# Experts of a gated mixture: high weights against high and low rows in one matmul, and a regrouped activation

## The reference

```python
h = jax.nn.silu(jnp.einsum('ech,ehi->eci', inp, wg)) * jnp.einsum('ech,ehi->eci', inp, wu)
out = jnp.einsum('eci,eih->ech', h, wd)
```

## Time and profile before

| | |
|---|---|
| median of three runs | 1830.35 us |
| the profiled execution | 1828.74 us |
| its span, first to last instruction | 1827.0 us |
| TensorE matmuls busy | 1797.5 us, 98% |
| VectorE busy | 1440.9 us, 79% |
| ScalarE busy | 1231.7 us, 67% |
| GpSimd busy | 1064.1 us, 58% |
| mean granted TensorE clock | 0.996 |

### The profile page before, as it was taken

One profiled execution on the slowest core, in us unless ns is written; L12 is line 12 of the kernel. 1 busy time (PEld: TensorE's weight loads), 2 busy tenths in 40 slices (PEclk: granted clock), 3 DMA queues, 4 the chain that ended last, 5 costly groups with the idle time before them and its releaser, 6 DMA issues.

```text
span 1827.0 us, 37430 instructions
## 1 busy us (share of the span) xinstructions
PE 1797.5 (98%) x13271; PEld 1323.8 (72%) x13335; DVE 1440.9 (79%) x2387; ACT 1231.7 (67%) x1799; POOL 1064.1 (58%) x813
## 2 busy tenths in 40 slices
PE   9999998999999999999999999999999999999997
PEld 4666667777777777777777777777777777777775
DVE  5999998787778787777777777777777787777772
ACT  6999997666666666666666666666666666666662
POOL 1101003767677767666666666667667767666651
PEclk9999999999999999999999999999999999999998
DMA  7677764999989999999999999999999999999982
GB/s 247 220 257 248 253 234 171 305 307 306 307 303 309 309 304 299 296 299 297 298 297 298 297 300 299 302 303 308 307 304 308 308 304 297 299 297 297 299 279 46
DMA packets 95817, 516.99 MB, mean 283 GB/s; under 512 B 17696, under 2 KB 22816, under 8 KB 71840
## 3 DMA queue, kind: packets, MB, share of 16 engines
q1 hardware_dynamic: 47968, 357.19, 49.2%
q0 software_dynamic: 42912, 151.04, 35.4%
q10 hardware_dynamic: 4896, 8.26, 1.6%
HBM read 409.21 MB, written 107.22 MB: 283 GB/s over the span
## 4 chain that ended last, share of the span: by engine, by line
PE 81%; DVE 2%; issue 1%; ACT 0%; DMA 0%; POOLq 0%; DVEq 0%; ACTq 0%
PE ps_gu L551 54%; PE ps_d L565 27%; DVE split_g L1161 0%; DVE split_u L1166 0%; DVE split_d L1171 0%; DMA xg<-h_rows,g_idx 0%; DVE xt L1187 0%; DVE xT L1192 0%; ACT ob L837 0%; PE ps_x L533 0%; PE ps_l L447 0%; ACT xT L817 0%; DVE prod L1179 0%; POOLq L106 0%; DVE act L1181 0%
## 5 line engine op out<-in xcount | busy, mean ns | idle before, releaser
L1333 POOL DMA_INDIRECT xg<-h_rows,g_idx x504 | 725.2, 1439 | 188.1 <-issue 134.1
L551 PE MATMUL ps_gu<-xT,split_g 128*128 128x256 bf16 x4608 | 534.1, 273 | 0.8 <-DVE xT L1221 0.8
L551 PE MATMUL ps_gu<-xT,split_u 128*128 128x256 bf16 x4608 | 534.1, 273 | 0.0
L565 PE MATMUL ps_d<-split_d,act 128*128 128x512 bf16 x2240 | 494.3, 379 | 5.4 <-DVE act L1181 1.5
L551 PEld LDWEIGHTS ps_gu<-xT,split_g 128*128 128x128 bf16 x4608 | 450.8, 98 | 66.6 <-issue 1.1
L551 PEld LDWEIGHTS ps_gu<-xT,split_u 128*128 128x128 bf16 x4608 | 450.9, 98 | 52.2
L565 PEld LDWEIGHTS ps_d<-split_d,act 128*128 128x128 bf16 x2304 | 225.1, 98 | 260.9 <-DVE act L1181 2.6
L837 ACT ACTIVATE ob<-ps_d,wcol 128x512 f32<-128x512 f32 x256 | 173.1, 688 | 337.7 <-PE ps_d L565 296.3
L1353 POOL DMA_INDIRECT out<-ob,s_idx x128 | 205.5, 1605 | 291.7 <-ACT ob L837 245.8
L1171 DVE TENSOR_TENSOR split_d<-raw_d,split_d 128x1536 bf16<-128x1536 f32 x128 | 219.2, 1754 | 94.0 <-ACT split_d L809 94.0
L1187 DVE STREAM_TRANSPOSE xt<-xg 128x512 f32<-128x512 f32 x252 | 163.9, 689 | 129.7 <-DMA xg<-h_rows,g_idx 129.7
(11 more groups left out here) (121 smaller groups left out, 1397.4 us busy)
## 6 DMA issues: line engine op xcount, KB each, us to landing
raw_d<-in_wd SPq DMA_DIRECT2D x63, 1536.0 KB
raw_g<-in_wg SPq DMA_DIRECT2D x62, 1536.0 KB
raw_u<-in_wu SPq DMA_DIRECT2D x62, 1536.0 KB
h_rows<-hrow SPq DMA_DIRECT2D x33, 640.0 KB, 3.5
xb<-in_x SPq DMA_DIRECT2D x32, 512.0 KB, 5.3
out<-xb SPq DMA_DIRECT2D x32, 512.0 KB, 3.8
xg<-h_rows,g_idx POOLq DMA_INDIRECT x504
ctx_sb<-in_ctxT SPq DMA_DIRECT2D x8, 512.0 KB, 6.1
```

What stands on the lines that cost most here:

```text
L551: mm = pe.matmul(ps_gu[m][:, t, :], w[:, wi, k, m * P:(m + 1) * P], xT[u][:, k, xi, :], start=(k == 0 and (wi, xi) == (0, 0)), stop=(k == ...
L565: mm = pe.matmul(ps_d[n][:], act[u][:, ai, m, half * P:(half + 1) * P], split_d[:, wi, m, c * NH:(c + 1) * NH], start=(m == 0 and (wi, ai) ...
L1333: p.indirect_dma_start(out=xg[u][:, g, :], out_offset=None, in_=h_rows, in_offset=bass.IndirectOffsetOnAxis(ap=g_idx[u][:, g:g + 1].bitcas ...
```

## The change

- In a gate or up half, the high weights now meet high and low rows in one matmul of 512 columns that fills a whole bank, high x high in its first 256 columns and high x low in the last. The third product, low x high, stays a matmul of 256 columns into the first half. A half is 8 matmuls of 512 and 8 of 256.
- So each half needs a bank: five banks `ps_gu` are used in turn, bank (2m + t) mod 5, and `ps_d` has three, piece 3 using the bank of piece 0. The last up half waits until the first gate is summed; piece 3 waits until piece 0 is read out.
- The two 256-column halves of a bank have to be summed. For the gate, ScalarE copies the second half to `sil` (`gate_part`), VectorE adds the first (`gate_sum`), and ScalarE applies silu to `sil` in place. For the up product, VectorE sums both halves with a `tensor_reduce` into `prod`, and multiplies `prod` by `sil` in place. gate and up halves now signal separately.
- VectorE's low parts of the next expert's gate weights all come after the third activation, ahead of those of the up weights; ScalarE's turned high parts 2 and 3 come after silu 1.
- 20 matmuls in place of 44 run on the identity before the first expert, the first turned rows go to other banks, and near the end of the attention two steps of VectorE for the router's weights go between steps of the routes.

```diff
@@ TensorE
+                if m == MI - 1 and t == 1:
+                    pe.wait_ge(gate_summed, MI * e + 1)
-                    for wi, xi in PAIRS:
-                        mm = pe.matmul(ps_gu[m][:, t, :], w[:, wi, k, m * P:(m + 1) * P], xT[u][:, k, xi, :],
...
+                    pe.matmul(out_ps[:].rearrange("p x c -> p (x c)"), w[:, 0, k, m * P:(m + 1) * P],
+                              xT[u][:, k].rearrange("p x c -> p (x c)"), start=(k == 0), stop=False)
+                    mm = pe.matmul(out_ps[:, 0], w[:, 1, k, m * P:(m + 1) * P], xT[u][:, k, 0], start=False, stop=(k == KH - 1))
+                mm.then_inc((gate_done, up_done)[t], 1)
...
                 for n in range(2, 4):
-                    if not first:
-                        pe.wait_ge(down_out, 4 * e - 3 + n)
+                    if n == 3:
+                        pe.wait_ge(down_out, 4 * e + 1)
...
-            for _ in range(44):
+            for _ in range(20):
@@ ScalarE
+            def gate_part(e, m, first=False):
+                s.wait_ge(gate_done, MI * e + m + 1)
+                if m == 0 and not first:
+                    s.wait_ge(act_ready, MI * e)
+                s.activation(sil[:, m], bank(m, 0)[:, 1], ACT.Copy).then_inc(gate_copied, 1)
             def silu(e, m):
-                s.wait_ge(gu_done, MI * e + m + 1)
-                s.activation(sil[:, m], ps_gu[m][:, 0], ACT.Silu, scale=H_SCALE).then_inc(sil_done, 1)
+                s.wait_ge(gate_summed, MI * e + m + 1)
+                s.activation(sil[:, m], sil[:, m], ACT.Silu, scale=H_SCALE).then_inc(sil_done, 1)
...
                 s.wait_ge(silu_table, 1)
+                gate_part(0, 0, True)
                 gate_high(1, 1, 0, True)
+                gate_part(0, 1, True)
                 gate_high(1, 1, 1, True)
+                silu(0, 0)
+                gate_part(0, 2, True)
                 up_high(1, 1, 0, True)
-                silu(0, 0)
+                silu(0, 1)
                 up_high(1, 1, 1, True)
-                silu(0, 1)
                 silu(0, 2)
                 for q in range(4):
                     turned_high(1, 1, q)
@@ VectorE
+            def gate_sum(e, m):
+                v.wait_ge(gate_copied, MI * e + m + 1)
+                v.tensor_tensor(sil[:, m], bank(m, 0)[:, 0], sil[:, m], ALU.add).then_inc(gate_summed, 1)
             def activate(e, u, m, first):
+                v.wait_ge(up_done, MI * e + m + 1)
+                chain.link(v.tensor_reduce(prod[:, m], bank(m, 1)[:].rearrange("p x c -> p c x"), mybir.AxisListType.X, ALU.add))
...
-                chain.link(v.tensor_tensor(prod[:, m], sil[:, m], ps_gu[m][:, 1], ALU.mult))
+                chain.link(v.tensor_tensor(prod[:, m], sil[:, m], prod[:, m], ALU.mult))
@@ VectorE, first expert
                 up_low(0, 0, 0)
                 up_low(0, 0, 1)
+                gate_sum(0, 0)
                 down_low(0, 0)
                 down_low(0, 1)
+                gate_sum(0, 1)
                 gate_low(1, 1, 0)
+                gate_sum(0, 2)
                 activate(0, 0, 0, True)
                 gate_low(1, 1, 1)
                 activate(0, 0, 1, True)
```

More of the change, by code:

```diff
@@ L292, in flamingo_moe, with bank @@
         p_mem.close()
-        ps_gu = [ps(f"ps_gu{m}", [P, 2, CAP], F32, ctx) for m in range(MI)]
-        ps_d = [ps(f"ps_d{i}", [P, NH], F32, ctx) for i in range(4)]
-        ps_x = ps("ps_x", [P, QS, 2, E], F32, ctx)
+        ps_gu = [ps(f"ps_gu{i}", [P, 2, CAP], F32, ctx) for i in range(5)]
+        ps_d = [ps(f"ps_d{i}", [P, NH], F32, ctx) for i in range(2)]
+        x_mem = ExitStack()
+        ps_x = ps("ps_x", [P, QS, 2, E], F32, x_mem)
+        x_mem.close()
+        ps_d.append(ps("ps_d2", [P, NH], F32, ctx))
+        def bank(m, t):
+            return ps_gu[(2 * m + t) % 5]
+        FIRST_TURNED = [ps_gu[1][:].rearrange("p x c -> p (x c)"), ps_gu[3][:].rearrange("p x c -> p (x c)"), ps_d[0][:], ps_d[1][:]]
         block = ctx.enter_context(nc.Block())
@@ L564, in down_part @@
                     for wi, ai in PAIRS:
-                        mm = pe.matmul(ps_d[n][:], act[u][:, ai, m, half * P:(half + 1) * P],
+                        mm = pe.matmul(ps_d[n % 3][:], act[u][:, ai, m, half * P:(half + 1) * P],
                                        split_d[:, wi, m, c * NH:(c + 1) * NH],
@@ L574, in down @@
                 pe.wait_ge(act_ready, MI * e + MI - 1)
+                if first:
+                    pe.wait_ge(pieces_made, 1)
                 for n in range(2):
                     if not first:
-                        pe.wait_ge(down_out, 4 * e - 3 + n)
+                        pe.wait_ge(down_out, 4 * e - n)
                     down_part(u, n, range(MI - 1))
@@ L851, in expert @@
                     gate_high(e + 1, 1 - u, 1, none_before)
-                    turned_high(e + 1, 1 - u, 2)
-                    turned_high(e + 1, 1 - u, 3)
+                gate_part(e, 1)
+                if not last:
                     weights(e + 1, 1 - u)
@@ L856, in expert @@
                 if not last:
+                    turned_high(e + 1, 1 - u, 2)
+                    turned_high(e + 1, 1 - u, 3)
+                gate_part(e, 2)
+                if not last:
                     up_high(e + 1, 1 - u, 0, none_before)
+                silu(e, 2)
+                if not last:
                     up_high(e + 1, 1 - u, 1, none_before)
-                silu(e, 2)
                 rows_out(e, u, first)
@@ L1199, in expert @@
                 down_low(e, 0)
+                gate_sum(e, 0)
                 down_low(e, 1)
+                activate(e, u, 0, first)
                 if not last:
@@ L1203, in expert @@
                     turned_low(e + 1, 1 - u, 1)
-                activate(e, u, 0, first)
+                gate_sum(e, 1)
                 if not last:
@@ L1207, in expert @@
                     turn(e + 1, 1 - u, 3)
-                    gate_low(e + 1, 1 - u, 0)
+                activate(e, u, 1, first)
+                if not last:
                     turned_low(e + 1, 1 - u, 2)
                     turned_low(e + 1, 1 - u, 3)
-                activate(e, u, 1, first)
-                if not last:
-                    gate_low(e + 1, 1 - u, 1)
+                gate_sum(e, 2)
                 activate(e, u, 2, first)
                 if not last:
+                    gate_low(e + 1, 1 - u, 0)
+                    gate_low(e + 1, 1 - u, 1)
                     up_low(e + 1, 1 - u, 0)
```

37 lines of the change are left out of this document (20 added, 17 removed).

## The result

The changed kernel takes 1826.31 us, median of 19 runs (1824.70 to 1828.81), beside 1829.87 for the kernel before (19 runs on the same chips). The ratio is 0.9982, 95% interval 0.9975 to 0.9988. So it is faster by 0.18%, which is 3.3 us (the two medians differ by 3.6): clearly not zero, but just inside the 0.2% that I had set for "no change". The forecast was 1827.7, in a range of 1820 to 1838.

What follows compares the result with a forecast made beforehand. TensorE's expert matmuls were taken to bound the kernel. From the profiled 1828.74: -7.6 + 6.9 - 2.4 - 0.3 + 0.8 = 1826.1; with the median 1.6 higher, 1827.7 us, range 1820 to 1838.

Steps and rivals of the forecast that it cites:

- TensorE, steady: Matmuls of every expert: merging 48 pairs saves 0.12 us, period 23.37, over 63 experts -7.6 us.
- rivals E and F: E: the merge saves nothing, 1835, chance 0.08; F: a merged matmul costs as little as one of 256, chance 0.01.
- VectorE's load and the reduce: Each block adds a gate sum, about 0.38 us, and a PSUM reduce near 0.69; VectorE's load becomes 21.5 us per expert.
- The third activation: Before down's block 2 in each expert: still covered by down's first 12 matmuls, cost 0, 0.1 us to spare.
- rival C: Third activation ends too late in each of 63 experts if the reduce exceeds about 0.85 us: 1834 to 1840, chance 0.13.
- The first expert: VectorE's longer queue and ScalarE's order stall TensorE; expert 1 starts at 339.65 against 332.79, +6.9 us.
- my three waits: TensorE in the first expert's down: 3.1 us for activation 1, 0.9 for activation 2, 2.9 for piece 0's read-out.
- Given back: Experts 1 and 2 no longer lose time to gathers and activations: 49.36 us become two periods, 46.98, -2.4 us.
- The router step: Before the first expert: router work put forward starts ScalarE's row shares sooner, -0.3 us, bounds 0 and -0.5.
- The clock: Half-clock stretches over the first gates and perhaps after the first expert's waits: +0.8 us, bounds 0 and +3.4.
- the chance of "faster": Time below 1826.7 us: four tenths of the forecast as worked out (0.58), plus two rivals; stated as 0.38.
- rival D: The lower clock catches both places, first gates and first expert's waits, in full: 1831 us, chance 0.08.

Runs made afterwards that it cites:

- x13: The kernel of x1 run again, unchanged, on the third chip: 1834.52 us (one run).
- x4: Changed kernel with the reduce of block 2 done twice in each expert, on the second chip: 1848.22 us (one run).
- x9: Changed kernel with 18 instead of 12 down matmuls before block 2 (more cover for the third activation), second chip: 1827.63 us, ratio 0.9986.
- x8: Changed kernel with VectorE's two low parts of the gate weights back ahead of activations 2 and 3, first chip: 1893.90 us (one run).
- x14: The kernel of x3 run again, unchanged, on the third chip: 1822.24 us, ratio 0.9957.
- x16: The kernel of x2 run again, unchanged, on the fourth chip: 1827.66 us, ratio 0.9989.
- x3: Changed kernel; in the first expert ScalarE reads out pieces 0 and 1 before the high parts of expert 1's rows; first chip: 1831.64 us, ratio 1.0008.
- x1: Changed kernel with each merged matmul taken apart into two of 256 columns, first chip: 1930.51 us, ratio 1.0549.
- x2: Changed kernel with 44 idle matmuls in place of 20, first chip: 1837.41 us, ratio 1.0045.
- x10: Changed kernel with the edits of x3 and x9 together, second chip: 1823.17 us, ratio 0.9959.
- x15: The kernel of x10 with 44 idle matmuls in place of 20, third chip: 1824.59 us, ratio 0.9969.

## Why the prediction was right

**TensorE, steady: right.** Period 23.37, forecast 23.37; x13 beside it, 23.49, isolates the merge (with its weight load) at 0.12 us per expert and refutes rivals E and F. In the table, 60 experts give the 7.2 us that 60 x 0.12 makes. The Trainium skill's rate (TensorE: Matmul & The Clock Gate, section "Back-to-back issue gap"), 131 ns, would have taken an estimated 4.2 us off each expert. It is not what this trace shows: its stream of loads and matmuls ran at 216 ns per 512 columns.

**VectorE's load and the reduce: right.** 681 ns for a taken 0.69, 21.30 us for 21.5. The estimate from the cycle table of the Trainium skill (VectorE: DVE Perf Modes, section "The TRN2 errata") was 658 ns. Its advice to restructure a reduce (same page, section "Rules for kernel authors") did not decide, as the reduce lay under the cover.

**The third activation: right, with more room than I gave it.** I put the margin at 0.1 us, the records say 0.23 and x4 says 0.38. x9 shows that more cover brings nothing, so rival C has no share in the result. (C's price counts what the reduce takes beyond 0.85 us; by my own sum it should have been beyond 0.69 + 0.1 = 0.79.) x8 shows what held it: without the move of the weight parts, the third activation ends too late, at 1.1 us per expert.

**The first expert: right in mechanism, 0.7 us too dear.** Of my three waits (3.1, 0.9, 2.9) the last two came as 0.72 and 2.80. The first was 2.3 in the executions where the gates ran at the full clock (x14 and x16). The term mis-sized is VectorE's queue. I had read it as at work without a gap, but before the change it stood idle 0.57 us for the first silu, which now is ready in time. I added six instructions and forgot to take that wait out. The six were a little cheaper too: a sum 0.33 and a reduce 0.71 us from start to start, where I had 0.38 and 0.725. The row of the kernel before, in VectorE's timeline:

```profile
320.40 0.42 DVE L1179 TENSOR_TENSOR prod<-sil,ps_gu 128x256 f32<-128x256 f32 x1 [0.57 <-ACT sil L813]
```

Expert 1 started at 338.95 instead of 339.65. x14 shows that the wait for the read-out comes from ScalarE's order alone: two instructions moved, and expert 1 starts at 336.28, 2.7 us earlier. From the start of down it takes 9.39 us instead of 11.63, and x3, whose down ran at the full clock, takes 8.66. Its median lies 4.1 us below that of the changed kernel. What the other 1.4 are (chip, clock or the router's end) was not parted.

**Given back: right.** Experts 1 and 2 take two plain periods, and the waits for gathers are gone.

**The router step: not shown.** In the profile the spread of the table starts 0.2 us earlier (298.96 against 299.15). But over the executions of the kernels with the same router it started anywhere from 298.5 to 302.5, so this says nothing. I did not try it alone.

**The clock: the mechanism, not the price, and in part luck.** I took +0.8 between 0 and +3.4. The profiled execution had the stretch where down waited anyway, at a cost of 0. Others had it over piece 3, at 1.4 us (x16) and 1.6 (x13). My value lies between, but for no better reason than that.

**The sum.** Against the profiled execution: 1826.1 forecast, 1825.18 measured. Up to the start of expert 1 the forecast was 6.9 - 0.3 + 0.8 = +7.4, measured +6.2; from there on -7.6 - 2.4 = -10.0, measured -2.6 - 7.2 = -9.8; and 0.1 lies outside the span. So the first part was 1.2 us too dear, made up of the 0.7 of VectorE's queue and the 0.8 of the clock, less a router step not shown to be there. The median of before came out at 1829.87 rather than 1830.35, which is the other 0.5. Two slips in the prediction's numbers change nothing: the chance of "faster" adds up to 0.36 (four tenths of 0.58, with 0.12 and 0.01), not 0.38, and rival D's time is 1827.7 + 2.6 = 1830.3, not 1831.

## What to carry to other kernels

- Of merged matmuls, the columns are the price; joining two saved only 2.6 ns each time. Such a change lives or dies by the work that it gives the other engines, and by the first pass, where nothing is covered yet: here the stall of one expert took back most of what 63 experts won.
- Order the queue of an engine by who waits for it. Two read-outs put ahead of four conversions, in one expert, brought as much as the whole change: x14's 1822.24 us is the best kernel here, 7.8 below the 1830.01 of the kernel before on the same chip.
- A control that misses its number by far more than any theory allows should first be run again on another chip, before a mechanism is built on it.

## What I had not expected of the hardware

**Late signals on one chip.** In the four kernels of the first chip, semaphore increments of the last matmul of a gate or up half came up to 3 us after the matmul's end (once 4), mostly in x1 (81 of 192 up signals over 0.5 us late), rarely in x2 and x3 (9 and 6 of those on record), and hardly in x8 (one, by 0.63, which nothing waited for). I found no such delay in the increments of down's last matmuls, nor in those of VectorE and ScalarE. Some records of signals are missing from those traces (of x1's gate signals 163 of 192 are there, its up signals are complete), so the other counts are rough; the starts of the waiting engines bear them out. On three other chips, eight kernels showed none, among them the same x1, x2 and x3 again. The kernel before took 1830.06 us on the first chip as well, no slower than elsewhere; it signals once per block. Whether the chip or the hour was at fault stays open, and whether the changed kernel itself would lose time on that chip was not tried. Its 19 runs show no such loss. A cover as in x10 costs little (1823.17 beside 1822.24, intervals overlapping) and would hide 1.3 us more of such a delay, but it was not run there.

**The clock after a wait.** A wait of TensorE of 2.8 us ahead of piece 3 was followed by half the clock in x1, x2, x13 and x16. In the profiles of the changed kernel, x4 and x8 the same wait was not. The wait of 2.27 us ahead of down was followed by it in x14 and x15, and not in x2, x3, x10 and x16. What decides is not shown.
